# Projections of a delta-rule stage from pairs of fp16 numbers in place of fp32

## What is computed

```python
h = _rms(x, attn_norm_w)
q = silu(silu(_causal_dwconv(h @ Wq.T, conv_q)))       # 512 x 512, four taps
k = silu(silu(_causal_dwconv(h @ Wk.T, conv_k)))
v = silu(silu(_causal_dwconv(h @ Wv.T, conv_v)))
q, k = _l2norm(q), _l2norm(k)                          # per head: 32 heads of 16
beta = jax.nn.sigmoid(h @ Wbeta.T)                     # 512 x 32
def step(S, inp):
    kt, qt, vt, bt = inp
    err = jnp.einsum('bhvk,bhk->bhv', S, kt) - vt
    S = S - bt[..., None, None] * err[..., None] * kt[..., None, :]
    o = jnp.einsum('bhvk,bhk->bhv', S, qt)
    return (S, o)
o = _rms(o.reshape(B, T, H), out_norm_w) @ Wout.T
```

## Time and profile before

| | us |
|---|---|
| median of three runs | 3256.35 |
| lowest, highest | 3254.93, 3263.09 |
| the profiled execution | 3251.3 |
| its span in the trace | 3249.3 |
| delta stage, first load to last instruction | 579 to 1762 |
| busy over the span: TensorE, VectorE, ScalarE, GpSimd | 2897.0, 1944.5, 1462.6, 1007.6 |
| mean granted clock of TensorE | 0.934 |

### The profile page before, as it was taken

How to read it: one execution, slowest core, us unless ns; L and a number is a source line. 1 busy time by engine, 2 the same in 40 slices (tenths; PEclk the granted TensorE clock), 3 DMA queues, 4 the chain that set the end, 5 groups by cost and what they waited for, 6 DMA issues and landing times. The chain is left out here.

```text
span 3249.3 us, 65853 instructions
## 1 busy us (share of the span) xinstructions
PE 2897.0 (89%) x26552; PEld 1541.2 (47%) x26552; DVE 1944.5 (60%) x2956; ACT 1462.6 (45%) x2438; POOL 1007.6 (31%) x710
## 2 busy tenths in 40 slices
PE   6999999587899988999844999999999699999997
PEld 3444444244454444444423444444444366666665
DVE  3444444259977978779891444445442466666665
ACT  2222222376665766757612422222222366666665
POOL 0000000125725527255290000000000267777776
PEclk9999999788989989989866999999999899999999
DMA  6998898200000000000003132322200111111010
GB/s 241 334 336 309 301 332 271 87 14 1 2 27 8 22 28 2 27 9 21 15 15 119 56 117 78 104 91 91 98 33 27 63 36 39 39 39 39 33 42 30
DMA packets 126423, 290.19 MB, mean 89 GB/s; under 512 B 30496, under 2 KB 35360, under 8 KB 122112
## 3 DMA queue, kind: packets, MB, share of 16 engines
q1 hardware_dynamic: 122752, 261.91, 23.0%
q10 hardware_dynamic: 3456, 25.17, 2.3%
HBM read 245.02 MB, written 42.01 MB: 88 GB/s over the span
## 5 line engine op out<-in xcount | busy, mean ns | idle before, releaser
L803 POOL TENSOR_TENSOR b_tmp<-b_L,b_U 128x496 f32<-128x496 f32 (+30 forms) x248 | 252.1, 1017 | 558.6 <-ACT b_L L1040 539.8
L1984 POOL TENSOR_TENSOR d_zb<-d_za 128x1024 f32<-128x1024 f32 x32 | 75.3, 2353 | 1047.0 <-DVE d_za L2040 1047.0
L845 PE MATMUL b_e<-b_hT,b_wqkv 128*128 128x512 f32 x768 | 367.8, 615 | 3.9 <-DVE b_raw L1223 3.1
L1273 DVE TENSOR_TENSOR b_U<-b_U,b_tmp 128x1488 f32<-128x1488 f32 (+30 forms) x248 | 282.2, 1138 | 8.6
L1271 DVE TENSOR_TENSOR b_tmp<-b_L,b_U 128x1488 f32<-128x1488 f32 (+30 forms) x248 | 265.3, 1070 | 32.3 <-ACT b_L L1040 26.4
L805 POOL TENSOR_TENSOR b_U<-b_U,b_tmp 128x496 f32<-128x496 f32 (+30 forms) x248 | 271.7, 1096 | 19.4
L1493 PE MATMUL c_r<-c_hT,c_g_pair 128*128 128x512 f16 x1056 | 255.5, 394 | 13.1 <-DVE c_hT L1658 13.1
L1223 DVE SCALAR_TENSOR_TENSOR b_raw<-b_e,b_cw,b_raw 128x496 f32<-128x496 f32 (+2 forms) x288 | 204.3, 717 | 99.2 <-ACT b_raw L1057 90.9
L1667 DVE SCALAR_TENSOR_TENSOR c_av<-c_r,c_sg 128x512 f32<-128x512 f32 x88 | 60.8, 691 | 305.3 <-PE c_r L1493 248.1
L1493 PE MATMUL c_r<-c_hT,c_u_pair 128*128 128x512 f16 x1056 | 242.7, 379 | 0.0
L1493 PE MATMUL c_d<-c_d_pair,c_aT 128*128 128x512 f16 x1056 | 241.0, 379 | 0.0
(11 more groups left out here) (229 smaller groups left out, 5486.1 us busy)
## 6 DMA issues: line engine op xcount, KB each, us to landing
a_cT<-in_ctxT SPq DMA_DIRECT2D x128, 512.0 KB, 9.6
a_cn<-in_ctx SPq DMA_DIRECT2D x128, 512.0 KB, 8.6
a_x_ln<-in_x SPq DMA_DIRECT2D x8, 1024.0 KB, 15.7
a_cw<-in_ctx SPq DMA_DIRECT2D x128, 64.0 KB, 9.2
a_x_res<-in_x SPq DMA_DIRECT2D x32, 256.0 KB, 11.1
x<-a_x_out SPq DMA_DIRECT2D x32, 256.0 KB, 10.9
b_xg<-x SPq DMA_DIRECT2D x8, 1024.0 KB, 5.4
om<-b_hT SPq DMA_DIRECT2D x32, 256.0 KB, 2.0
```

The costliest lines, as they stand in the source:

```text
L803: nc.gpsimd.tensor_tensor(tmp[:, QV, s + 1:S, :], lo, us, ALU.mult).then_inc(pool_prod, 1)
L845: mm = pe.matmul(p[:], w_qkv[:, i, n, c * P:(c + 1) * P], hT[:, n, :], start=(n == 0), stop=(n == DC - 1))
L1273: V.tensor_tensor(U[:, 0:QV, s + 1:S, :], U[:, 0:QV, s + 1:S, :], tmp[:, 0:QV, s + 1:S, :], ALU.subtract).then_inc(sub, 1)
L1984: nc.gpsimd.tensor_tensor(o[:, :, 0, :], a[:, :, 0, :], a[:, :, 1, :], ALU.add).then_inc(bf, 1)
```

## The change

Each of the weights for q, k, v and beta is kept as two fp16 numbers: `high` is the weight times 256 rounded to fp16, `low` the rest. The rows are kept so too, times 64. A projection is then three fp16 matmuls for each fp32 one: high by high, high by low, low by high. The factor 256 x 64 is taken out in `cw` and in the scale of beta's Tanh.

The high half of the rows is written by ScalarE in place of the fp32 copy (the same four instructions of 128x512). The low half is a new instruction on VectorE, `low_rows`, four for each group: for group 0 ahead of everything, for group g+1 after step 24 of pass k. VectorE now frees the four banks of `rows`. The weights are loaded into `raw` and `Up`, split by ScalarE and VectorE, and GpSimd's memset of `Up` comes after that, between its scaling of `vec` and `cw` (new) and that of `w_o`.

```diff
@@ the weights, staged
-        w_qkv = sb("wqkv", [P, 3, DC, D])
-        w_b = sb("wb", [P, DC, NH])
+        w_qkv = sb("wqkv", [P, 2, 3, DC, D], F16)
+        w_b = sb("wb", [P, 2, DC, NH], F16)
...
-        hT = hT_all[:].rearrange("p (c n) -> p c n", n=GT)
+        hp = hT_all[:].bitcast(F16).rearrange("p (i c n) -> p i c n", i=2, n=GT)
...
+        WS, HS = 256.0, 64.0
+        STAGED = tuple((raw_all[:, i * DC * D:(i + 1) * DC * D], src.rearrange("p c n -> p (c n)"),
+                        w_qkv[:, :, i].rearrange("p j c n -> p j (c n)")) for i, src in enumerate((wq, wk, wv)))
+        STAGED += ((Up[:, 0:DC * NH], wbeta.rearrange("p c n -> p (c n)"), w_b[:].rearrange("p j c n -> p j (c n)")),)
@@ GpSimd, at the start
-            nc.gpsimd.memset(Up[:], 0.0).then_inc(zeroed, 1)
             pool.wait_ge(loaded, 16 * len(LOADS))
+            nc.gpsimd.tensor_scalar(hvec[:], vec[:, 0], HS, None, ALU.mult).then_inc(vec_ready, 1)
+            nc.gpsimd.tensor_scalar(cw[:], cw[:], 1 / (WS * HS), None, ALU.mult).then_inc(vec_ready, 1)
+            pool.wait_ge(w_ready, len(STAGED))
+            nc.gpsimd.memset(Up[:], 0.0).then_inc(zeroed, 1)
@@ TensorE
             pe.wait_ge(wo_ready, DC)
+            pe.wait_ge(w_ready, len(STAGED))
...
                 for n in range(DC):
-                    mm = pe.matmul(p[:], w_qkv[:, i, n, c * P:(c + 1) * P], hT[:, n, :],
-                                   start=(n == 0), stop=(n == DC - 1))
+                    for a, b in ((0, 0), (0, 1), (1, 0)):
+                        mm = pe.matmul(p[:], w_qkv[:, a, i, n, c * P:(c + 1) * P], hp[:, b, n, :],
+                                       start=(n + a + b == 0), stop=(n == DC - 1 and a == 1))
@@ ScalarE
+            act.wait_ge(loaded, 16 * len(LOADS))
+            for src, _, pair in STAGED:
+                A.activation(pair[:, 0], src, ACT.Copy, scale=WS).then_inc(w_hi, 1)
             act.wait_ge(zeroed, 1)
-            act.wait_ge(loaded, 16 * len(LOADS))
+            act.wait_ge(vec_ready, 2)
...
-                    p, free = E.take(act, 0, f"{g}.h{c}")
-                    A.activation(hT[:, c, :], p[:], ACT.Copy, scale=vec[:, 0, c:c + 1]).then_inc(free, 1)
+                    p, _ = E.take(act, 0, f"{g}.h{c}")
+                    A.activation(hp[:, 0, c, :], p[:], ACT.Copy, scale=hvec[:, c:c + 1]).then_inc(h_hi, 1)
@@ VectorE
+            for i, (src, _, pair) in enumerate(STAGED):
+                dve.wait_ge(w_hi, i + 1)
+                V.scalar_tensor_tensor(pair[:, 1], src, WS, pair[:, 0], ALU.mult, ALU.subtract).then_inc(w_ready, 1)
             dve.wait_ge(zeroed, 1)
+            dve.wait_ge(vec_ready, 2)
+
+            def low_rows(g):
+                for c in range(DC):
+                    p, free = E.take(dve, 0, f"{g}.h{c}")
+                    dve.wait_ge(h_hi, g * DC + c + 1)
+                    V.scalar_tensor_tensor(hp[:, 1, c, :], p[:], hvec[:, c:c + 1], hp[:, 0, c, :],
+                                           ALU.mult, ALU.subtract).then_inc(free, 1)
...
+                if g == 0:
+                    low_rows(0)
                 for s in range(S - 1):
                     if cur:
                         solve(k, s)
+                    if s == 24 and g + 1 < NG:
+                        low_rows(g + 1)
```

More of the change, by code:

```diff
@@ L689, in delta_phase @@
         vec = sb("vec", [P, 2, DC])
+        hvec = sb("hvec", [P, DC])
         ident = sb("ident", [P, P])
@@ L703, in delta_phase @@
         hT_all = sb("hT", [P, DC * GT])
-        hT = hT_all[:].rearrange("p (c n) -> p c n", n=GT)
+        hp = hT_all[:].bitcast(F16).rearrange("p (i c n) -> p i c n", i=2, n=GT)
         ov = hT_all[:].rearrange("p (t d) -> p t d", d=D)
-        raw = sb("raw", [P, DC, 3, GT])
+        raw_all = sb("raw", [P, DC * 3 * GT])
+        raw = raw_all[:].rearrange("p (c i n) -> p c i n", i=3, n=GT)
         stat = sb("stat", [3 * NH, GT])
@@ L729, in delta_phase @@
         loaded, eps_ready, wo_ready, zeroed = sem("loaded"), sem("eps"), sem("wo"), sem("zeroed")
+        w_hi, w_ready, vec_ready, h_hi = sem("w_hi"), sem("w_ready"), sem("vec_ready"), sem("h_hi")
         x_ready, hn_ready = sem("x_ready"), sem("hn_ready")
@@ L741, in delta_phase @@
         block = stack.enter_context(nc.Block())
-        LOADS = ((w_qkv[:, 0], wq), (w_qkv[:, 1], wk), (w_qkv[:, 2], wv), (w_b[:], wbeta), (w_o[:], wout),
-                 (cw[:], conv), (vec[:], vecs), (ident[:], consts["ident"]), (heads[:], consts["heads"]),
+        LOADS = tuple((dst, src) for dst, src, _ in STAGED) + (
+                 (w_o[:], wout), (cw[:], conv), (vec[:], vecs), (ident[:], consts["ident"]), (heads[:], consts["heads"]),
                  (spread[:], consts["spread"]), (own[:], consts["own"]), (past[:], consts["past"]),
@@ L786, in _ @@
             nc.gpsimd.memset(eps[:], RMS_EPS).then_inc(eps_ready, 1)
+            pool.wait_ge(loaded, 16 * len(LOADS))
+            nc.gpsimd.tensor_scalar(hvec[:], vec[:, 0], HS, None, ALU.mult).then_inc(vec_ready, 1)
+            nc.gpsimd.tensor_scalar(cw[:], cw[:], 1 / (WS * HS), None, ALU.mult).then_inc(vec_ready, 1)
+            pool.wait_ge(w_ready, len(STAGED))
             nc.gpsimd.memset(Up[:], 0.0).then_inc(zeroed, 1)
-            pool.wait_ge(loaded, 16 * len(LOADS))
             for c in range(DC):
@@ L836, in betas @@
                 for c in range(DC):
-                    mm = pe.matmul(p[2 * NH:3 * NH, :], w_b[:, c, :], hT[:, c, :], start=(c == 0), stop=(c == DC - 1))
+                    for i, j in ((0, 0), (0, 1), (1, 0)):
+                        mm = pe.matmul(p[2 * NH:3 * NH, :], w_b[:, i, c, :], hp[:, j, c, :],
+                                       start=(c + i + j == 0), stop=(c == DC - 1 and i == 1))
                 mm.then_inc(full, 1)
@@ L1051, in betas @@
                 act.wait_ge(vt_ready, DC * (k + 1))
-                A.activation(stat[2 * NH:3 * NH, :], p[2 * NH:3 * NH, :], ACT.Tanh, scale=0.5).then_inc(free, 1)
+                A.activation(stat[2 * NH:3 * NH, :], p[2 * NH:3 * NH, :], ACT.Tanh, scale=0.5 / (WS * HS)).then_inc(free, 1)
             def tap_first(g, name, c):
```

## The result

| | us |
|---|---|
| kernel before, median (lowest to highest) | 3257.93 (3254.93 to 3263.09) |
| changed kernel, median (lowest to highest) | 3223.23 (3222.68 to 3225.42) |
| ratio of the medians, 95% interval | 0.9893 (0.9876 to 0.991) |
| profiled executions, before and changed | 3251.3, 3223.2 |
| their spans | 3249.3, 3221.4 |

The changed kernel is faster by 34.7 us, 1.07%. The forecast was 3235, in a range of 3219 to 3251.

The account below looks back on a forecast made before the run. TensorE looked like the bound, with VectorE only some 25 us slack per solve. Start +13.3, lead-in -11, low halves +17.4, waits -45.6, contention +2.5 and clock +2 gave -21.4: profiled 3230, median 3235, range 3219 to 3251.

Parts of the forecast that it names:

- the two kinds of wait: VectorE's waits before the convolutions (26.6 us) and before each group's first scaling (19.0) both vanish: -45.6 us.
- (c): Spreads and later scalings: the clock recovers before the spreads, later waits shrink 2 us in each of six solves; 3223, chance 0.12.
- start 13.3, lead-in -11: Before solve 0: weight splitting and memset delay the stage start, +13.3 us; thirteen shorter products in the lead-in save 11.
- Low halves: VectorE after step 24 of solves 0 to 5: four new instructions, 2.9 us a set, passed on in full, +17.4.
- TensorE's wait for q1's bank: TensorE before q3 in solve 3: the PSUM bank of q1 is free at 1121.5, once q1 is convolved.
- Contention: VectorE's solve steps slow beside GpSimd's: between nothing and 1 us in each of six solves, +2.5 taken.
- The clock: TensorE at the spreads: a short new wait may prolong the low clock, 0 to 2 us in each of six; +2.
- The dip at q0: TensorE's clock drop at a group's first projection, after waiting for low halves, is hidden by the wait for q1's bank.
- From profile to median: Whole kernel: the profiled execution, 5 us below the median of the runs, would take 3230; the median becomes 3235.
- (a): TensorE up to the spreads can't hand its gain on; half of the 45.6 us of waits stays: 3253, chance 0.14.
- (b): Projections: after the low-halves wait the clock stays at the 1.2 GHz level; with five such projections 3291, chance 0.07.
- (d): Whole delta stage: TensorE is the bound all along, so its full 87 us saving counts: 3182, chance 0.03.

## Why the prediction was right, and where it was off

VectorE became the bound up to the spreads, and the two kinds of wait went, as forecast; that mechanism is what was right. The median of 3223 lies in the range, but just under the 3226 to 3244 of the forecast itself, and it is the time that rival (c) gave. That is a coincidence: what (c) describes hardly happened. By the first profiled execution of each kernel:

| term | forecast | measured |
|---|---|---|
| start 13.3, lead-in -11 | +2.3 | +0.4 |
| solve 0, one set of low halves | +2.9 | +2.8 |
| solves 1 to 6 | -26.6 | -30.7 |
| solve 7 and the last output | 0 | +2.7 |
| the stages after | 0 | -3.1 |
| sum | -21.4 | -27.9 |

The third row is 14.5 (five sets) - 45.6 + 2.5 + 2. The last two are differences between single executions: in the second profile of the changed kernel solve 7 and the output take 141.7, as before the change (141.4).

**Start: right.** 12.5 later against the loads, with the memset between the low halves and `w_o`. The loads themselves came 1.0 sooner. The lead-in gave back 11.1 where 11 was forecast, and the 0.8 before the first projection lies in it.

**Low halves: right.** 20 records of 0.745 us, 13.6 in all for five sets where 14.5 was taken. Left out, a set gives 1.7 to 2.1 us outside the third scaling's wait, and VectorE idles 0.6 to 1.0 in its place: together the 2.7 that VectorE spends on it.

**Waits: right, for a reason that was only half of it.** Both kinds vanished, as worked out. b_stat was ready 62.7 us after the start of the solve (62.4 forecast: 1159.4 against a start at 1097.0), and TensorE was early by 3.4 us and not by 1.5, since the outer products started at 47.6 us and ended at 59.3 (48.3 and 60.9 forecast). TensorE's wait for q1's bank is seen only where q0 comes early: in solve 3 of the run without low halves it is 1.53 and ends at 24.6 us (24.5 forecast). But the text treats the kernel before as bound by TensorE with VectorE's idle time as slack. The run with four more instructions on VectorE shows that most of it wasn't slack: 2.9 us of each 3.33 came through. Had the change added its low halves without making TensorE faster, they would have cost about as much.

**Contention: right size.** VectorE's 372 instructions of the solve itself took 208.2 + 192.7 = 400.9 us, before 398.1: 2.8 more, where 2.5 was taken. With the low halves at step 30, where VectorE waits at its convolutions again, they took 395.2. So they are slower the less VectorE waits; that GpSimd is the cause was argued, and no run took it away.

**The clock: wrong sign.** +2 was taken, because a new wait could lengthen the dip. The later waits went from 77.5 to 76.6 instead. The third scaling waits 11.3, 8.1, 10.0, 8.1, 10.3 and 6.5 us in solves 1 to 6 of the kernel before and 10.5, 8.1, 8.1, 10.4, 8.1 and 8.1 in the changed one: shorter in three, the same in one, longer in two. So no steady effect of the earlier outer products is seen. This term was 2.9 us off. The dip at q0 is hidden as the text has it, as long as it is short: with 6.7 to 7.0 us for q0 and k0 the outer products start 47.6 us into solves 2, 3, 5 and 6, and with 5.35 and no dip there (the run without low halves) they start at 47.5. In solve 4 the dip is longer and they start 2.8 later; there the margin at the spreads hides it.

**From profile to median: the largest error.** The sum gave 3230 for the profiled execution, and 5 us were added because the median of the runs lay 5 above it. The second profile of the kernel before suggests what these 5 us are: the waits at the convolutions and the first scaling, 50.4 us there and 45.6 in the first. That is what the change removes, so it should not have been added again. No profile of the runs at 3255 to 3263 shows it directly. The spread of the runs agrees: those of the kernel before on all chips lie between 3240.5 and 3263.1, those of the changed kernel between 3219.2 and 3225.4. In the run with the low halves behind step 30, where such waits are back, ten runs lie between 3238.5 and 3253.1. Of the 11.8 us between forecast and result 5 are this, and 6.5 the terms of the table.

**The rivals.** (a) needed waits of 4 us before the first scaling: there was none. (b) needed a clock under 0.8 over the stretch from q0 to v3: from q0 to the outer products it is 0.97 in solve 3 and 0.92 in solve 4. Yet solve 4 shows that its mechanism is there: behind the wait of 3.03 the clock costs 2.9 us at q0 and k0 and 1.6 at beta, and the margin at the spreads hides it. The run with step 30 is what (b) was about: there such a loss comes in five solves of six, and with the delay itself the margin is used up and the gain gone. (c) is not seen: it needed later waits under 6 us, and the third scaling, the longest of them, waits 8.1 or more. (d) is excluded: with a third of the products the solves keep their length.

## What to carry to other kernels

Where two engines wait for each other once per round, idle time need not be slack on either: ask at which point each is late, and test it with a few idle instructions on the one that is to take over work. Work put on the engine that becomes the bound is paid in full, but its place can be moved as long as the other engine still waits somewhere; that wait (3.44 us here) is the margin, and it has to cover a low clock behind the new wait too, which can come in one solve and not in the next. If the waits that a change removes vary from run to run, the distance from the profiled run to the median goes with them.
